# Summing the last two chunks of the second layer's relation weights on VectorE instead of TensorE

## What is computed

```python
def rgcn_gate_layer(x, row, col, edge_type, basis, att, gate_w, root, bias):
    w = jnp.einsum('rb,bio->rio', att, basis)      # [2, 512, 512] from [2, 30] and [30, 512, 512]
    x_j = x[col]
    msgs = []
    for r in range(2):
        gate = jax.nn.sigmoid(x_j @ gate_w[r, :, 0])
        msgs.append(gate[:, None] * x_j @ w[r])
    msg = jnp.where((edge_type == 0)[:, None], msgs[0], msgs[1])
    agg = jax.ops.segment_sum(msg, row, num_segments=x.shape[0])
    return agg + x @ root + bias

h = jax.nn.relu(rgcn_gate_layer(x, ..., basis1, att1, gate_w1, root1, bias1))
out = rgcn_gate_layer(h, ..., basis2, att2, gate_w2, root2, bias2)
```

## Time and profile before

| | |
|---|---|
| time, median of 3 runs | 502.21 us (501.56 to 502.63) |
| the profiled execution's own time | 500.15 us |
| its span | 498.4 us |
| TensorE (PE) busy | 456.5 us, 92% |
| VectorE (DVE) busy | 218.0 us, 44% |
| ScalarE (ACT) busy | 166.8 us, 33% |
| GpSimd (POOL) busy | 177.7 us, 36% |
| the parts' matmuls, L1661, 512 records | 66.0 us |
| HBM read, written | 103.92 MB, 14.82 MB |

### The profile page before, as it was taken

How to read it: one execution, slowest core, us unless ns; L and a number is a source line. 1 busy time by engine, 2 the same in 40 slices (tenths; PEclk the granted TensorE clock), 3 DMA queues, 4 the chain that set the end, 5 groups by cost and what they waited for, 6 DMA issues and landing times.

```text
span 498.4 us, 7432 instructions
## 1 busy us (share of the span) xinstructions
PE 456.5 (92%) x2602; PEld 321.5 (65%) x2602; DVE 218.0 (44%) x527; ACT 166.8 (33%) x365; POOL 177.7 (36%) x201
## 2 busy tenths in 40 slices
PE   2799799979999999798999999999999999999993
PEld 2344356768765665466667788777777877775772
DVE  5779981322262626553313002333002658853445
ACT  2799763322220111831205004225006360133320
POOL 3101200055230541199061790622404625940522
PEclk9999999999999999999999999999999999999986
DMA  5999999868999978964910816040002193999646
GB/s 126 380 427 417 429 423 362 345 249 311 369 399 412 383 256 322 422 256 179 315 47 2 250 44 252 1 108 1 5 1 64 42 336 101 272 343 359 209 156 196
DMA packets 38788, 119.27 MB, mean 239 GB/s; under 512 B 7050, under 2 KB 7111, under 8 KB 30302
## 3 DMA queue, kind: packets, MB, share of 16 engines
q1 hardware_dynamic: 33406, 111.30, 59.8%
q0 software_dynamic: 3360, 3.86, 3.2%
q10 hardware_dynamic: 1984, 3.61, 1.9%
HBM read 103.92 MB, written 14.82 MB: 238 GB/s over the span
## 4 chain that ended last, share of the span: by engine, by line
PE 75%; DMA 7%; issue 5%; DVE 3%; ACT 3%; POOL 2%; SPq 2%; DVEq 1%; POOLq 0%; ACTq 0%
PE ps L1637 14%; PE ps L1639 13%; PE ps L1638 13%; PE ps L1661 9%; PE ps L1996 9%; DMA ring<-in_L_gnn_basis_dram 4%; PE ps L1722 3%; DMA y_dram<-ybuf 2%; PE ps L2131 2%; PE ps L2121 2%; PE ps L1841 2%; ACT h_tmp L1374 1%; PE ps L1645 1%; POOL piece_lo L746 1%; DMA got<-y_dram,slot_u 1%
## 5 line engine op out<-in xcount | busy, mean ns | idle before, releaser
L1661 PE MATMUL ps<-ring,sel_att 128*32 128x512 f32 x512 | 66.0, 602 | 6.5 <-DMA ring<-in_L_gnn_basis_dram 3.0
L1637 PE MATMUL ps<-piece_hi,ht_hi 128*125 128x512 f32 x140 | 56.1, 401 | 0.8 <-PE ps L1639 0.6
L1097 DVE SCALAR_TENSOR_TENSOR u_lo<-ps,gates,u_hi 125x512 fp32r<-125x512 f32 x20 | 15.0, 751 | 94.1 <-ACT u_hi L1520 94.1
L1638 PE MATMUL ps<-piece_lo,ht_hi 128*125 128x512 f32 x140 | 55.1, 394 | 0.0
L1639 PE MATMUL ps<-piece_hi,ht_lo 128*125 128x512 f32 x140 | 55.1, 394 | 0.0
L745 POOL CAST piece_hi<-piece_raw 128x512 fp32r<-128x512 f32 x28 | 19.8, 707 | 91.9 <-issue 53.7
L746 POOL TENSOR_TENSOR piece_lo<-piece_raw,piece_hi 128x512 fp32r<-128x512 f32 x28 | 37.8, 1350 | 13.4 <-issue 11.2
L947 DVE TENSOR_SCALAR oh_n<-iota_n,keys 125x626 f16<-125x626 f16 x100 | 37.8, 378 | 8.1 <-PE ps L1722 6.1
L1996 PE MATMUL ps<-u_hi,cf 125*125 125x512 f32 x100 | 39.9, 399 | 1.3 <-PE ps L1639 1.3
L1996 PE MATMUL ps<-u_lo,cf 125*125 125x512 f32 x100 | 39.4, 394 | 0.0
L1722 PE MATMUL ps<-oh_n,oh_m 125*128 125x313 f16 x200 | 31.4, 314 | 4.0 <-DVE oh_m L948 3.9
(11 more groups left out here) (334 smaller groups left out, 929.7 us busy)
## 6 DMA issues: line engine op xcount, KB each, us to landing
ring<-in_L_gnn_basis_dram SPq DMA_DIRECT2D x64, 1024.0 KB, 8.0
w_home<-in_L_ffn_W_sp_dram SPq DMA_DIRECT2D x27, 256.0 KB, 6.5
rel_dram<-stag SPq DMA_DIRECT2D x16, 256.0 KB, 7.9
w_raw<-rel_dram SPq DMA_DIRECT2D x8, 512.0 KB, 6.8
w_fq<-in_L_ffn_W_fq_dram SPq DMA_DIRECT2D x2, 2048.0 KB, 10.7
y_dram<-ybuf ACTq DMA_DIRECT2D x13, 256.0 KB, 4.5
piece_raw<-in_L_mix_Wkqv_dram SPq DMA_DIRECT2D x3, 1024.0 KB, 9.4
x_dram<-stag SPq DMA_DIRECT2D x1, 3072.0 KB
```

What stands on the lines that cost most here:

```text
L1097: dve.scalar_tensor_tensor(out=u_lo[l][:, t, :], in0=ps[0:TP, u_bank(i), :], scalar=gates[:, t, r:r + 1], in1=u_hi[l][:, t, :].bitcast(F32 ...
L1637: pe.matmul(target, a_hi, b_hi, start=first, stop=False, skip_group_check=skip)
L1638: pe.matmul(target, a_hi, b_lo, start=False, stop=False, skip_group_check=skip)
L1661: last = pe.matmul(ps[32 * c:32 * c + 32, rel_bank(ch), :], sel_att[:, ch // CHUNKS, g].rearrange("p r q -> p (r q)"), ring[slot][:, c * D ...
```

## The change

The factors of the second layer are also loaded, spread over all partitions, as `att_all` [128, 60]. Chunks 14 and 15 are no longer cut into parts (TensorE's parts go from 64 to 56, ScalarE's copies from 16 to 14). Instead SyncE loads their rows of each basis with two loads of 128 KB, 60 loads in all, into the four buffers `ring` 0 to 3, four bases to a buffer, in two turns. For each basis and relation VectorE does one step: `stag[r] = ring * factor + stag[r]`, 128x512, both inputs in SBUF; the first of each relation is a `tensor_scalar`. That is 60 steps. The first 32 (bases 0 to 15) alternate between the relations. Then come 14 steps of relation 0, then 14 of relation 1, and each of these waits for the one before it. The steps lie between VectorE's others as written out here. Each relation is stored (`store_sum`, two stores of 128 KB) and read back (`read_second`, four loads of 256 KB) by itself, after the loads of `root2` and `x_again`, which now come earlier in SyncE's order.

```diff
@@ loads and stores, SyncE
+            def load_for_vector(turn, s):
+                if turn == 0:
+                    sp.wait_ge(basis_used, PARTS - 4 + s + 1)
                 else:
+                    sp.wait_ge(basis_used, PARTS + s + 1)
+                for b in V_OF[s]:
+                    if b // 16 == turn:
+                        for c in range(V_CHUNKS):
+                            sp.dma_start(ring[s][c * QI * KT:(c + 1) * QI * KT, b % 4 * D:(b % 4 + 1) * D],
+                                         basis_v[b, CHUNKS - V_CHUNKS + c]).then_inc(basis_in[s], 16)
+
+            def store_sum(r):
+                sp.wait_ge(rel_evac, P_CHUNKS + r + 1)
+                for c in range(V_CHUNKS):
+                    sp.dma_start(rel_dram[1][:, r, :, CHUNKS - V_CHUNKS + c, :].rearrange("t q n -> q t n"),
+                                 stag[c * QI * KT:(c + 1) * QI * KT, r, :]).then_inc(rel_out[r], 16)
+
+            def read_second(r):
+                if r == 0:
+                    sp.wait_ge(rel_out[1], 16 * (P_CHUNKS // 2))
                     sp.wait_ge(split_done, PIECE["rel1_1"] + 1)
+                sp.wait_ge(rel_out[r], 16 * (P_CHUNKS // 2 + V_CHUNKS))
                 for t in range(KT):
+                    sp.dma_start(w_raw[:, t, r, :], rel_dram[1][t, r].rearrange("q c n -> (q c) n")).then_inc(rel_back[t], 16)
...
+            load_for_vector(0, 0)
+            load_for_vector(0, 1)
+            store_chunk(P_CHUNKS - 2)
+            load_for_vector(0, 2)
+            load_for_vector(0, 3)
+            store_chunk(P_CHUNKS - 1)
+            load_piece("root2")
             sp.wait_ge(hT_t, NT)
             for a, b in ROWS:
                 sp.dma_start(x_again[a:b, :, :], x.rearrange("(t p) n -> p t n", p=TP)[a:b]).then_inc(x_in, 16)
-            read_relations(1)
+            for s in range(4):
+                load_for_vector(1, s)
+            for r in range(REL):
+                store_sum(r)
+                read_second(r)
@@ VectorE
+            SUMS = [(b, r) for b in range(16) for r in range(REL)] + [(b, r) for r in range(REL) for b in range(16, BASES)]
+            def sums(count):
+                for b, r in SUMS[summed[0]:summed[0] + count]:
+                    s, turn_, target = b // 4 % 4, b // 16, stag[:, r, :]
+                    dve.wait_ge(basis_in[s], 16 * (V_AT[s] + V_CHUNKS * len([a for a in V_OF[s] if a // 16 <= turn_])))
+                    source, factor = ring[s][:, b % 4 * D:(b % 4 + 1) * D], att_all[:, r * BASES + b:r * BASES + b + 1]
+                    if b == 0:
+                        dve.wait_ge(rel_out[r], 16 * (P_CHUNKS // 2))
+                        step = dve.tensor_scalar(target, source, factor, None, ALU.mult)
+                    else:
+                        dve.wait_ge(dve_own, last_of[r])
+                        step = dve.scalar_tensor_tensor(out=target, in0=source, scalar=factor, in1=target, op0=ALU.mult, op1=ALU.add)
...
+                    if b < 16 and b % 4 == 3 and r == REL - 1:
+                        dve.sem_inc(basis_used, 1)
+                    if b == BASES - 1:
+                        dve.sem_inc(rel_evac, 1)
...
             for t in range(NT):
+                sums(2)
                 dve.wait_ge(w2_mm, t + 1)
@@ def messages(l), VectorE
+                if l == 0:
+                    sums(3)
                 dve.wait_ge(gate_mm, l + 1)
                 dve.tensor_copy(in_halves(gate_row[:]), ps[0:2 * REL, 0:2, 0:HALF]).then_inc(gate_row_ready, 1)
+                if l == 0:
+                    sums(6)
                 dve.wait_ge(gates_ready, l + 1)
...
                         dve.scalar_tensor_tensor(out=u_lo[l][:, t, :], ...).then_inc(u_ready, 1)
+                        if l == 0 and r == 0:
+                            sums(2)
+                    if a == 0:
+                        sums(len(SUMS) - summed[0])
@@ GpSimd, def split(name)
-                        pool.wait_ge(rel_back[t], 16 * (l + 1))
+                        pool.wait_ge(rel_back[t], 16 * (l + 1 + l * r))
@@ TensorE
             turn_xn(0)
-            relation_parts(1)
             s, p_hi, p_lo = piece("W2")
...
                 if t + 1 < NT:
                     turn_xn(t + 1)
-                relation_parts(1)
...
                 if l == 0:
-                    relation_parts(PARTS - part[0])
+                    assert part[0] == PARTS
                     pe.wait_ge(xm_ready, 3)
                 else:
-                    pe.wait_ge(rel_evac, 2 * CHUNKS)
+                    pe.wait_ge(rel_evac, P_CHUNKS)
```

More of the change, by code:

```diff
@@ L47 @@
 CHUNKS = D // QI // 4
-PARTS = 2 * CHUNKS * NG
+V_CHUNKS = 2
+P_CHUNKS = 2 * CHUNKS - V_CHUNKS
+PARTS = P_CHUNKS * NG
 WIDE = 6 * NG
@@ L199, in gnn_mix_ffn @@
         kq_lo = place("kq_lo", [128, KT, NPAD], F32R, r_u + KB628)
+        att_all = place("att_all", [128, REL * BASES], F32, r_bias + 5 * D * 4 + 1024)
         y = place("y", [TP, NT, D], F32, r_u)
@@ L319, in gnn_mix_ffn @@
         w_in, router_in = sem("w_in"), sem("router_in")
[L320 to L323, removed]
+        w2_in, W2_SEEN = [w_in, edges_in, att_in, smalls_in, rel_back[2]], [16, 48, 32, 176, 48]
+        w1_fq_in, W1_FQ_SEEN, w1_moved, w1_moved_dve = rel_back[0], 48, sem("w1_moved"), sem("w1_moved_dve")
+        V_AT = [WIDE // 8 + (PARTS - WIDE) // 4] * 4
+        V_OF = [[b for b in range(BASES) if b // 4 % 4 == s] for s in range(4)]
+        RING_SEEN = [V_AT[s] + V_CHUNKS * len(V_OF[s]) for s in range(4)] + [3] * 4
+        y_out, Y_SEEN = (basis_in[0:3], basis_in[3:8]), [[16 * RING_SEEN[i] for i in r] for r in (range(3), range(3, 8))]
+        w2_fq_in, W2_FQ_SEEN = rel_back[1], 48
         k_hi_done = sem("k_hi_done")
@@ L476, in rel_bank @@
         def rel_bank(ch):
-            return 3 + ch % 2 if ch < 2 * CHUNKS - 2 else 3
+            return 3 + ch % 2 if ch < P_CHUNKS else 3
         def y_buf(b, i):
@@ L552, in _ @@
                 load_part(i)
-            piece_after = {11: "k", 24: "q", 27: "v", 30: "Wo", 34: "W1", 40: "W2", 50: "root1", 62: "root2"}
+            piece_after = {11: "k", 24: "q", 27: "v", 30: "Wo", 34: "W1", 40: "W2", 50: "root1"}
             chunk = 0
@@ L556, in _ @@
                 load_part(i)
-                while chunk < 2 * CHUNKS and i >= min(NG * chunk + (12 if NG * chunk + 12 <= WIDE else 9), PARTS - 1):
+                while chunk < P_CHUNKS - 2 and i >= min(NG * chunk + (12 if NG * chunk + 12 <= WIDE else 9), PARTS - 1):
                     store_chunk(chunk)
@@ L756, in _ @@
                 split(name)
-            pool.wait_ge(smalls_in, 16 * 5)
+            pool.wait_ge(smalls_in, 16 * 6)
             own_step(pool.tensor_tensor(bias_row[:, 4, :], bias_row[:, 4, :], bias_row[:, 1, :], ALU.add))
@@ L775, in _ @@
             for s in rel_out:
-                pool.wait_ge(s, 16 * CHUNKS)
+                pool.wait_ge(s, 16 * (P_CHUNKS // 2 + V_CHUNKS))
             pool.memset(stag[:, 0, :], 0.0).then_inc(consts_ready, 1)
```

34 lines of the change are left out of this document (19 added, 15 removed).

## The result

The changed kernel takes 514.61 us, the median of 4 runs (513.36 to 515.34), beside 502.42 (501.56 to 503.38) for the kernel before on the same chip. The ratio is 1.0239, 95% interval 1.0209 to 1.0270. I had forecast 504.8 us, with a range up to 508.0. So the sign was right, while the size was wrong: + 12.2 us measured, + 2.6 forecast.

What follows compares the result with a forecast made beforehand. TensorE was taken to set the end, with room on VectorE. - 6.0 at the gates, + 2.8 for nine sums and + 5.8 for the long run made + 2.6 us: median 504.8 us, range 498.5 to 508.0.

Steps and rivals of the forecast that it cites:

- Step 1: W2 to the gates: with the parts gone from TensorE, the gates start at about 248.5, 6.0 us earlier.
- the part ahead of it is only filler, so W2 starts where it did: Start of W2: removing the part ahead changes nothing, W2 still starts at 230.36 behind act_lo.
- catches up: W2 loop: VectorE, with two steps more a tile, falls behind in one tile at most and recovers; cost nothing.
- Step 2: Cost of one sum on VectorE: 0.66 us unhindered, two per GpSimd cast and subtraction 2.8 us, one per addition 1.76 us.
- Rival (b): Milder: sums pass GpSimd's additions at 1.35 us, or dependent sums start 0.75 us apart; 501.2 to 503.2 us, 20 in 100.
- the price of sums that depend on each other: The last 28 sums on VectorE: each starts 0.79 us after the one it waits for.
- Step 3: Nine sums at the gates delay the first u_lo, so relation 0's third tile waits: 2.8 us lost.
- Step 4: 33 sums ahead of relation 1's first u_lo outlast TensorE's cover, so its third tile waits: 5.8 us lost.
- the other 21 alone at 0.79 us, 16.6 us: Last 21 sums of the long run, after GpSimd's split and additions: they run unhindered until 305.4.
- Step 5: Store, read-back and split of relation 0 end at 319.2, before layer 2's first tile at 329.2; nothing lost.
- (c): Sums hardly held up, under 0.88 us each on average in the long run, all 6.0 us stay; 496.2 us, 20 in 100.
- (d): Loads or the way back are late, 3 us more on some sums; 507.8 us, 10 in 100.

Runs made afterwards that it cites:

- the changed kernel with the filler: The complete changed kernel plus four matmuls of no use in the wait for act_lo ahead of W2; 512.57 us, ratio 1.0229.
- the second experiment: The changed kernel with both relations stored before either is read back, order of the sums unchanged; 511.99 us, ratio 1.0179.
- the last versions: Changed kernel, sums alternating, relation 1 in PSUM, part 55 moved ahead of W2: 497.21 us; then two gate sums moved into W2: 496.26 us.
- no sums, filler again: Rerun of the changed kernel without 58 of 60 sums, with four useless matmuls ahead of W2; 496.53 us, ratio 0.9905.

## Why the prediction was right and wrong

**Step 1, the gates: nearly right.** 5.3 us of the 6.0 were gained between W2 and the gates, and the wait of 1.46 us for `ht_lo` at the gates is the one that the prediction uncovered (1.4 us). What failed is a clause: "the part ahead of it is only filler, so W2 starts where it did". It does start there, but the part had kept the wait at 1.39 us. Without it TensorE is idle for 2.38 us and runs its first seven matmuls of W2 0.43 us apart instead of 0.23, and the tile takes 4.27 us up to its transposition, where the changed kernel with the filler has 2.86: 1.4 us. Against it stands an error the other way: a tile without its part takes 3.24 us, not the 3.43 of the forecast, so five take 0.8 us less.

```profile
237.17 0.47 PE L1709 MATMUL ps<-piece_hi,act_hi 128*125 128x512 f32 x1
...
240.41 0.47 PE L1709 MATMUL ps<-piece_hi,act_hi 128*125 128x512 f32 x1
```

The two make up the missing 0.7 us. In the changed kernel with the filler the leg is 18.15 us (231.17 to 249.32), almost the 18.14 of the forecast (230.36 to 248.5), but by chance: the full clock and the short tiles alone would give less, and the second tile takes 0.6 us more there, 0.44 of it a wait for `ht_lo`.

The second sum waited 3.39 us for the store of chunk 13, whose issue stood behind 16 loads in SyncE's queue. I had not seen this wait. It cost nothing here: VectorE had idle time again at 246.7, before the gates. With the filler, where TensorE is sooner, it is behind the 0.44 us just named. So "catches up" and the price of nothing were right by luck, since W2's first tile was slow.

**Step 2, turns with GpSimd: right.** A sum alone takes 0.75 us, beside the split a pair takes 2.7 us (five took 6.77 us), where 2.8 were forecast, and beside the additions one gets through per addition (5 additions in 8.42 us, 1.7 each; forecast 1.76). GpSimd can lose out too: its subtraction at 255.90 took 3.31 us instead of 1.28, while three sums in a row ran beside it (255.99, 2.06 us), so the turns are not kept in every case. Rival (b), 1.35 us beside the additions, is refuted, and with it the estimate of 503.4. Wrong was the price of sums that depend on each other: 0.855 us apart, not 0.79. The pair that I had taken it from the earlier trace rows was two different steps.

**Step 3, the gates' nine sums: right.** The wait is 2.44 us, forecast 2.8. Not in the sum was the half clock behind it: seven matmuls 0.43 us apart, about 1.5 us more. Together they are most of the + 4.15 us of that leg.

**Step 4, the long run: the mechanism right, the term mis-sized.** 33 sums lay ahead of `u_lo`, as counted. The first twelve ended at about 292.6 (5, and 7 of the next 14), 18 us behind their start at 274.64; forecast were 18.4 us (270.4 to 288.8). The failed term is "the other 21 alone at 0.79 us, 16.6 us". They took 21.1 us:

- The last 8 lay beside the split of `rel2_0`: 9.82 us instead of 8 x 0.79 = 6.3 (row below). That is + 3.5 us, of which 3.1 go when the split is moved away (the second experiment).
- 13 ran alone, but 0.065 us slower than assumed: + 0.8 us.

VectorE's timeline of the changed kernel from 303.9 us on:

```profile
303.98 9.82 DVE L1135 SCALAR_TENSOR_TENSOR stag<-ring,att_all,stag 128x512 f32<-128x512 f32 x8
```

That makes + 4.3 of the 4.5 us by which the leg missed its + 5.8.

**Step 5, the way back: "nothing" was the step that failed.** I checked only whether the read-back could be too late, and took the landing times of before, 7.9 and 6.8 us, medians over the whole kernel, most of them taken while the bases stream in. With the loads done, the store was in place in under 3.0 us (298.70 to 301.64) and the read-back in 2.7 us (301.64 to 304.35). So GpSimd's split began at 304.35, not at 311 or later, and it fell on the sums that TensorE was to wait for. Early was the costly side here. The row was right, but it was for a busy queue and for transfers of twice the size (256 and 512 KB, here 128 and 256 KB); no run parts the two.

**Left out altogether: the clock.** Behind the wait of 10.14 us fourteen matmuls ran at 1.2 GHz. This is the whole leg of + 2.7 us between relation 1's third tile and layer 2 (14 x 0.2 us). With 1.4 at W2 and 1.5 at relation 0 the half clock takes about 5.6 us in this trace, nearly half of the 11.9. The forecast had 8.6 us of waits in it and priced none of them with it, although all its own waits were idle time of TensorE. The price is not fixed: in the changed kernel with the filler only six matmuls ran at 1.2 GHz behind the wait of 10.12 us at the same place, about 1.3 us instead of 2.7. The waits themselves were taken away in the last versions, so what the clock costs of the kernel's time at relation 1 was not measured apart.

By the sum: forecast + 2.6; + 4.3 for the 21 sums; + 5.6 for the clock; - 0.8 for W2's shorter tiles; + 0.2 for the rest. This gives + 11.9, the measured + 11.9 of the four legs. The remaining 3.3 us lie ahead of W2 and behind layer 2's start, in these two profiled executions; the medians show at most 0.3 of them.

**Rivals.** (c) named the right condition, less than 0.88 us a sum. At 0.855 us alone even the dependent sums would meet it; it was GpSimd that they could not. (d), late loads, did not occur: no gap between sums was ended by a load, and the 60 loads landed in 2.8 us (median) each.

## What to carry to other kernels

Before work is moved to an idle engine, look at what lies beside it in time, not only at how much room it has: here VectorE was empty just where GpSimd, with which it shares SBUF access, was full. Price the same step by its operands: with the accumulator in PSUM the sum costs 0.75 us beside GpSimd, with it in SBUF one gets through in 1.7 us. Landing times measured on larger transfers under load were more than twice those of the quiet queue here, so ask of every transfer that is freed what happens if it lands early as well; and put a price on the clock behind each wait of TensorE that a sum contains, as a range: here 1.3 to 2.7 us.

## What the runs showed of the hardware

- **Turns in SBUF.** A VectorE step of 0.75 us with both inputs in SBUF mostly takes its turn between GpSimd's instructions: pairs of sums beside a cast and a subtraction take 2.7 us, and one sum passes per addition of 1.7 us. GpSimd pays as well: casts 0.95 us instead of 0.61, subtractions 1.6 us instead of 1.28, once 3.31 us beside three sums in a row.
- **Dependence.** Steps with a semaphore from one to the next start 0.855 us apart, steps that alternate between two accumulators 0.66 us (e.g. 279.75 and 280.40 above).
- **The half clock.** In the stretch of the change the granted clock was at 1.2 GHz after TensorE had been idle for 2.28 to 10.14 us, either at once or within 1.4 us of its restart, and stayed so for 2.7 to 6.1 us; behind idle times of 1.37 to 1.72 us it stayed at 2.4 GHz there. The length of the idle time alone doesn't decide it: elsewhere in the same traces the clock stayed full behind 2.34 us (the kernel before, at 111.73) and 3.03 us (no sums, filler again, at 112.19), was at half behind 3.23 us at the same product of the changed kernel, and fell behind 1.42 us with relation 1 in PSUM (at 208.35), where it stayed full in the kernel before (at 206.95). The stretches behind the restarts at 112.19 and 208.35, in this order:

```profile
112.19:115.19 3.00, 3.00 (x20) 3.00 (x21) 0.00 (x0) 0.00 (x0) 2.76 (x4) 1.00 0.57 134
```
```profile
208.35:211.35 3.00, 3.00 (x13) 1.01 (x14) 1.10 (x2) 2.97 (x8) 0.00 (x0) 0.52 1.01 429
```

- **Store and read-back.** Two stores of 128 KB and four loads of 256 KB, one after the other through HBM, took 5.65 us together with nothing else in the queues, where the medians of before, for transfers of twice the size and mostly under load, would give 14.7. How much of that is size and how much load was not measured.
